# Cross-attention and a routed expert layer: the second norm moves to ScalarE, and block 0 goes ahead of the last attention slot

## What is computed

```python
def reference(x, ctx_1024, mask, Wq, bq, Wk, bk, Wv, bv, norm_scale, w_router, w_up, w_down):
    x = x + xattn(layernorm(x), ctx_1024, mask, Wq, bq, Wk, bk, Wv, bv)
    return x + ffn(layernorm(x), norm_scale, w_router, w_up, w_down)

def ffn(x, norm_scale, w_router, w_up, w_down):
    xn = x * norm_scale * rsqrt(mean(x ** 2) + 1e-6)
    scores = xn @ w_router.T
    top, idx = top_k(scores, 2)
    weights = softmax(top)
    u, gate = split(moe_linear(xn, idx, w_up))
    down = moe_linear(u * silu(gate), idx, w_down)
    return sum(down * weights) + x
```

## Time and profile before

| | |
|---|---|
| median of 3 runs | 450.25 us (450.22 to 450.42) |
| the profiled execution | 450.19 us |
| its span, first to last instruction | 448.3 us |
| PE busy | 396.9 us (89%) |
| DVE busy | 345.0 us (77%) |
| ACT busy | 267.5 us (60%) |
| POOL busy | 252.8 us (56%) |
| mean granted TensorE clock | 0.964 |

### The profile page before, as it was taken

The page is one execution under the profiler, slowest core; times in us unless marked ns, Lnnn a source line. Parts: engine busy times, 40 slices in busy tenths (PEclk is TensorE's granted clock), DMA queues, the critical chain, the costliest instruction groups (busy, mean ns, idle before and its releaser), DMA issues. The chain is left out here.

```text
span 448.3 us, 10369 instructions
## 1 busy us (share of the span) xinstructions
PE 396.9 (89%) x2742; PEld 361.5 (81%) x2742; DVE 345.0 (77%) x1453; ACT 267.5 (60%) x642; POOL 252.8 (56%) x347
## 2 busy tenths in 40 slices
PE   2598999999999999999999999777989999999960
PEld 1598999999999999999999989756878788888750
DVE  2486888898898898898898898655776676777772
ACT  1165666656656656656656645424757677777750
POOL 1063244566566566566566574436777766566670
PEclk9989999999999999999999999776999999999995
DMA  4954473483483483483483350231223643338526
GB/s 125 326 150 171 166 264 95 162 281 97 171 280 105 165 283 104 164 283 107 159 284 111 154 168 21 59 86 30 74 84 102 158 117 87 84 90 285 193 67 217
DMA packets 60824, 68.66 MB, mean 153 GB/s; under 512 B 6096, under 2 KB 52320, under 8 KB 60768
## 3 DMA queue, kind: packets, MB, share of 16 engines
q1 hardware_dynamic: 56192, 58.52, 40.7%
q0 software_dynamic: 4544, 9.38, 6.3%
q10 hardware_dynamic: 32, 0.10, 0.1%
HBM read 54.41 MB, written 13.57 MB: 152 GB/s over the span
## 5 line engine op out<-in xcount | busy, mean ns | idle before, releaser
L1280 PE MATMUL ps<-attention,ctx_sb 128*128 128x128 f32 (+1 forms) x832 | 116.4, 282 | 10.5 <-ACT attention L704 4.8
L1280 PEld LDWEIGHTS ps<-attention,ctx_sb 128*128 128x128 f32 (+1 forms) x832 | 103.6, 195 | 17.7 <-issue 11.2
L631 POOL DMA_INDIRECT parts<-mbias,blk_x x78 | 77.8, 997 | 39.7 <-ACT mbias L771 31.5
L704 ACT ACTIVATE attention<-ps 128x512 f32<-128x512 f32 x96 | 56.5, 597 | 36.4 <-PE ps L1262 32.4
L537 POOL TENSOR_TENSOR rstd<-ve,minus_half 128x2 f32<-128x2 f32 x32 | 26.8, 837 | 90.0 <-DVE ve L894 90.0
L574 POOL DMA_INDIRECT rows_in<-kept,place x64 | 67.5, 1054 | 13.2 <-issue 12.7
L1262 PE MATMUL ps<-ident,attention 128*128 128x128 f32 (+1 forms) x416 | 68.4, 281 | 0.0
L838 DVE CUSTOM_DVE_ANT_0 attention<-ps,mbias 128x1608 f32<-128x1608 f32 x32 | 58.6, 1830 | 4.3 <-issue 4.3
L678 ACT ACTIVATE attention<-attention,ebias 128x1601 f32<-128x1601 f32 x32 | 52.0, 1624 | 10.9 <-DVE ebias L856 10.7
L1185 DVE SCALAR_TENSOR_TENSOR ctx_sb<-ctx_sb,ps 128x256 f32<-128x256 f32 x78 | 32.8, 420 | 33.0 <-ACT ctx_sb L758 32.2
L1246 PE MATMUL ps<-ctxt_high,gt_high 128*128 128x402 f32 x128 | 48.3, 378 | 5.0 <-DVE ctxt_low L980 3.0
(11 more groups left out here) (132 smaller groups left out, 828.4 us busy)
## 6 DMA issues: line engine op xcount, KB each, us to landing
ctxt_in<-ctx_cols SPq DMA_DIRECT2D x16, 800.5 KB
mbias<-mbias_dram SPq DMA_DIRECT2D x16, 800.5 KB, 5.7
ctx_sb<-ctx_rows SPq DMA_DIRECT2D x16, 768.0 KB
blk_x<-rows_in SPq DMA_DIRECT2D x78, 65.0 KB, 1.9
attention<-parts SPq DMA_DIRECT2D x8, 512.0 KB, 5.2
x_in<-x SPq DMA_DIRECT2D x16, 128.0 KB, 4.7
wup_in<-w_up_t SPq DMA_DIRECT2D x8, 256.0 KB, 5.1
out<-base_all SPq DMA_DIRECT2D x8, 256.0 KB, 3.1
```

Source lines behind the costliest of these rows:

```text
L631: pool.indirect_dma_start(parts, bass.IndirectOffsetOnAxis(ap=blk_x[:, m % XR, D:D + 1].bitcast(I32), axis=0), blk_y[:, m % YR], None).the ...
L704: act.activation(probs_t[:, g * BANK:(g + 1) * BANK], ps_turn[:, g % 2], ACT.Copy).then_inc(s_pt_act, 1)
L1280: last = pe.matmul(ps_o[:, 0:P], ctx_sb[0:n, j, t], probs_t[0:n, t * P:(t + 1) * P], start=t == 0, stop=t == KT - 1)
```

## The change

Three things are done at once.

1. **The second norm.** Instead of three passes of DVE and one of POOL over a row, ACT makes both rows with one activation each, out = scale * x1 + bias with a scale and a bias per token: the normalised row straight into kept (`norm_unit`, twice 128 values) and the skip sum (`add_skip`). The coefficients are made on POOL behind the power: shift2, the roots times minus the mean (128x2), and scale2, the root plus one (128x1). DVE makes minus the mean (128x1), and the two variances in one instruction instead of two. norm_unit(u - 2) is ACT's first work in slot u, and PE now turns kept instead of xn2. norm_scale goes into the router weights, once, by DVE ahead of slot 0 (PE waits for it, `s_wr`), and into the up weights as they are split; norm_scale is loaded as 128x1 instead of 128 copies of its row.
2. **Smaller ones on DVE.** The logits aren't copied any more: `best` and `best_index` read them in PSUM, both ahead of the big maximum instead of behind it, and what waited for the copy (`s_lg`) now waits for the index. The two choices are marked by one instruction instead of two (`gates_hot`). The last expert's up weights are split in slot 30 instead of 31.
3. **The order.** Slot 31, the last one with attention, comes behind step 0, and the three behind it behind steps 2, 5 and 8 instead of 1, 4 and 7; the last ranking goes from step 10 to 11. PE's waits for the last turned probabilities go from `before_steps` to step 2. The blocks' hidden rows lie in the mask's buffer instead of that of the context, which slot 31 still reads.

```diff
-    LATE_SLOTS = [1, 4, 7]
-    LAST_RANK = 10
+    LATE_SLOTS = [0, 2, 5, 8]
+    LAST_RANK = 11
...
-        inner = ctx_sb[:].rearrange("p a t d -> p (a t d)")[:, 0:4 * 2 * H].rearrange("p (s j h) -> p s j h", s=4, j=2)
+        inner = mbias[:].rearrange("p a n -> p (a n)")[:, YR * D:YR * D + 4 * 2 * H].rearrange("p (s j h) -> p s j h", s=4, j=2)
...
-            for u in range(UNITS):
+            for u in range(UNITS - 1):
                 slot(u // 4, u % 4)
             before_steps()
             for m in range(NB + 3):
                 step(m)
                 if m in LATE_SLOTS:
-                    slot(PAIRS, LATE_SLOTS.index(m))
+                    u = UNITS - 1 + LATE_SLOTS.index(m)
+                    slot(u // 4, u % 4)
...
             def slot_first(i, k):
                 u = 4 * i + k
-                if is_unit(u - 2):
-                    pool.wait_ge(s_y, u - 1)
-                    pool.tensor_tensor(base_all[:, bass.ds(u - 2, 1)],
-                                       x1[:, (k - 2) % 4:(k - 2) % 4 + 1], y[:, (k - 2) % 2:(k - 2) % 2 + 1],
-                                       ALU.add).then_inc(s_base, 1)
...
                     pool.wait_ge(s_ve2, u)
-                    wait(pool, s_xn2, u - 1)
-                    pool.tensor_tensor(rstd2[:], ve2[:], minus_half[:], ALU.pow).then_inc(s_rs2, 1)
+                    wait(pool, s_xn2, u - 2)
+                    wait(pool, s_base, u - 2)
+                    pool.tensor_tensor(rstd2[:, j], ve2[:], minus_half[:], ALU.pow).then_inc(s_rs2, 1)
+                    pool.wait_ge(s_rs2, u)
+                    pool.wait_ge(s_mm, u)
+                    pool.tensor_tensor(shift2[:, j], rstd2[:, j], minus_mean[:].broadcast_to([P, 2]), ALU.mult)
+                    pool.tensor_tensor(scale2[:, j], rstd2[:, j, 0:1], ones[:, 0:1], ALU.add).then_inc(s_coef, 1)
...
+            def norm_unit(u):
+                act.wait_ge(s_coef, u + 1)
+                if u >= KEPT:
+                    act.wait_ge(s_scat[u % KEPT], 16 * TOP_K * (u // KEPT))
+                act.activation(kept[:, u % KEPT, :, 0:D], x1[:, u % RING:u % RING + 1].broadcast_to([P, TOP_K, D]),
+                               ACT.Identity, bias=shift2[:, u % 2, 1:2], scale=rstd2[:, u % 2, 1:2]).then_inc(s_xn2, 1)
+            def add_skip(u):
+                act.activation(base_all[:, u], x1[:, u % RING], ACT.Identity, bias=shift2[:, u % 2, 0:1],
+                               scale=scale2[:, u % 2]).then_inc(s_base, 1)
...
+                if is_unit(u - 2):
+                    norm_unit(u - 2)
                 if k % 2 == 1 and is_unit(u + 3):
                     split_ctxt(i + 1, k // 2)
...
                     act.activation(xnt[:, k % 2], ps_misc[:, 0:P], ACT.Copy).then_inc(s_rtc, 1)
-                    act.activation(kept[:, (u - 2) % KEPT, :, 0:D], xn2[:, k % 2:k % 2 + 1].broadcast_to([P, TOP_K, D]),
-                                   ACT.Copy).then_inc(s_keep, 1)
+                    add_skip(u - 2)
...
-                dve.tensor_scalar(ve2[:, 0:1], mv2[:, 1:2], LN_EPS, None, ALU.add)
-                dve.tensor_scalar(ve2[:, 1:2], mv2[:, 1:2], 1.0 + RMS_EPS, RMS_EPS * LN_EPS, ALU.mult,
-                                  ALU.add).then_inc(s_ve2, 1)
+                dve.scalar_tensor_tensor(ve2[:], ve_mul[:], mv2[:, 1:2], ve_add[:], ALU.mult, ALU.add).then_inc(s_ve2, 1)
+                dve.tensor_scalar(minus_mean[:], mv2[:, 0:1], -1.0, None, ALU.mult).then_inc(s_mm, 1)
-            def ln2_centre(i, kk):
-            def ln2_norm(i, kk):
-            def rms_norm(i, kk):
-            def take_logits(i, kk):
...
-                dve.max(top[:], logits[:]).then_inc(s_top, 1)
+                dve.max(top[:], ps_misc[:, 0:E]).then_inc(s_top, 1)
...
-                dve.max_index(top_i[:], top[:], logits[:]).then_inc(s_topi, 1)
+                dve.max_index(top_i[:], top[:], ps_misc[:, 0:E]).then_inc(s_lg, 1)
...
-                if k == 3 and is_unit(u):
+                if k == (3 if i < PAIRS - 1 else 2) and is_unit(u):
                     split_up_weights(i)
...
                 if is_unit(u - 2):
-                    take_logits(i, k - 2)
+                    best(i, k - 2)
+                    best_index(i, k - 2)
                 if is_unit(u + 1):
                     maximum(*following)
...
             ln1(0, 1)
             dve.wait_ge(s_consts, N_CONSTS)
+            dve.tensor_scalar(wr_sb[:], wr_in[:], norm_col[:], None, ALU.mult).then_inc(s_wr, 1)
...
-                    pe.transpose(ps_misc[:, 0:P], xn2[:, (k - 2) % 2], ident[:]).then_inc(s_rt, 1)
+                    pe.transpose(ps_misc[:, 0:P], kept[:, (u - 2) % KEPT, 0, 0:D], ident[:]).then_inc(s_rt, 1)
...
             pe.wait_ge(s_consts, N_CONSTS)
+            pe.wait_ge(s_wr, 1)
...
                 if is_block(m - 2):
                     pe.wait_ge(s_h, m - 1)
+                    if m == 2:
+                        pe.wait_ge(s_pt_dve, UNITS)
+                        pe.wait_ge(s_pt_act, 3 * UNITS)
...
                 pe.wait_ge(s_max, UNITS)
-                pe.wait_ge(s_pt_dve, UNITS)
-                pe.wait_ge(s_pt_act, 3 * UNITS)
                 pe.wait_ge(s_owner, 1)
                 load_owners(0)
                 turn_block(0)
```

102 lines of the change are left out of this document (45 added, 57 removed).

## The result

The change makes the kernel **slower: 460.14 us** (458.23 to 460.92, 4 runs) against 450.34, a ratio of 1.020 [1.017, 1.024]. The forecast was 454.1 us with a range to 458.0: right in its sign, short by 6 us. The profiled execution took 460.92 us, 10.7 more than that of before, its span 459.2.

A forecast was written before the change was run, and what follows sets the result against it. PE was taken to set the time, through its waits and clock. Start 2.5, attention slots -2.0 and boundary 3.4 gave +3.9 on 450.2: 454.1 us, spread 451.5 to 456, to 458 with low clock and late coefficients.

The forecast's parts named there:

- Start: Slot 0: PE's scores for unit 1 wait for scaled router weights, 4.1 us later, less 1.6 us: +2.5 us.
- the bound on POOL's small operations: Coefficients on POOL: its two new small operations take at most 226 ns each, from a 128x8 sum.
- The rival of late coefficients: Attention slots: POOL's small ones take twice their bound, PE waits some 0.1 us at 30 places, +3 us; chance 0.10.
- Attention slots: Even slots: the next queries' turn starts 0.17 us earlier in 12 slots, -2.0 us; L995's 3.5 us stay.
- ACT's price: ACT's two new activations add 0.64 us per unit, 20 us in all, costing PE nothing while two covers hold.
- Boundary: Slot 30's end to block 6's products: 34.0 us against 30.6, with 10.3 us idle for block 0: +3.4 us.
- waits of PE for the activation that writes kept: Sign that the prediction is wrong: PE waiting for ACT's normalised row.
- Behind that, the shift stays.: Behind block 6: PE is busy throughout, so the delay stays as it is.
- The low clock: Boundary rival: the clock stays low after the 10.3 us idle stretch, +3.0 us, 457.1 us; chance 0.18.
- The covered start: Start rival: the start's wait is covered, so its 2.5 us fall away, 451.6 us; chance 0.10.
- the faster case: Even slots: DVE's relief reaches both PE waits, 6.7 us instead of 2.0, giving 449.4 us; chance 0.10.
- The early load: Boundary rival: block 0 is loaded early, so the slot hides nothing, 10.3 us less, 443.8 us; chance 0.05.

The follow-up runs named there:

- second trace of the change: The change as it is, run again beside other kernels: 460.39 us, ratio 1.019.
- early row: Against the change, ACT makes the normalised row of the three late slots ahead of the block step before the slot: 457.16 us, 1.014.
- early load: Against the change, the row ends are signalled by themselves and only block loads wait for the owners: 451.62 us, 1.003.
- repaired split: Against the change, DVE's split of the context in slots 2 and 4 waits for POOL's coefficients: 456.22 us, 1.016.
- PE kept busy: Against the change, 60 products of the unit matrix while PE waits for block 0: 459.71 us, 1.017; with 46 products 457.90 us, 1.017.
- 46 products with the early row: The change with the late slots' row made early on ACT and 46 unit-matrix products while PE waits for block 0: 456.05 us, 1.013.
- the half that paid: The new normalisation alone, in the old order, against the kernel before: 449.85 us, 0.999; with both start repairs 447.15 us, 0.992.
- the other half: The kernel before with only the new order of slots and blocks and what it needs: 455.77 us, 1.013.

## Why the prediction was right in sign and wrong in size

- **Start, forecast +2.5.** The first steps hold: PE at 26.00 (26.2 forecast), slot 2 late by 2.6. What failed is the bound on POOL's small operations, 226 ns each. Two of them took 1.42 and 1.57 us beside the split, and slots 2 and 4 gave 1.3 us more. The row of a 128x8 sum gave the time of such an operation alone. I looked at what DVE has ahead of the coefficients, not at what it does beside them. (In the second trace of the change it is worse, 2.1 us, by the power of 2.79 us.) The rival of late coefficients thus came true in 2 slots and not in 30: in the other even slots the row never made PE wait.
- **Attention slots, forecast -2.0.** An even slot took 0.18 us less (0.17 forecast), and the waits at L995 kept their 3.5 us. With two odd slots of 7.96 and 8.09 us instead of 7.68, slot 6 to the end of slot 30 gave back 1.5 us. The rule that I weighed against it, the Trainium skill's cycles for a PSUM source (VectorE: DVE Perf Modes, The TRN2 errata), shows nothing here: MAX8 and the index, now from PSUM, took 0.17 us each, against 0.17 and 0.16 from SBUF.

```profile
214.21 0.17 DVE L928 MAX8 top<-ps 128x8 f32<-128x8 f32 x1 [0.16 <-issue]
...
214.50 0.17 DVE L933 FIND_INDEX8 top_i<-top,ps 128x8 uint32<-128x8 f32 x1
```

- **ACT's price.** 595 and 483 ns for the two activations (0.59 and 0.46 forecast), 19.1 us in all (20 forecast). That its covers hold was right until slot 30, but for slots 2 and 4 (waits of 0.34 and 0.39 us), and wrong behind it.
- **Boundary, forecast 34.0 us to block 6's products, +3.4.** It took 321.85 - 285.07 = 36.8 us, +6.2. Term by term: idle 10.6 (10.3); two turns and block 0's products 3.15 (2.6); the row 0.96 (1.0); slot 31 7.9 (8.3); from block 2's turn on **14.1 (11.8)**. The step that failed: "Less work of DVE in slot 32 and two blocks in flight take off most of the 3.15 us and the low-clock window behind it, about 4.5 us." They took off 2.2, so this term was 2.3 us too small. I had seen that slot 31's row stands on ACT behind a block step and counted 1.0 us for it; slots 32 and 33 have the same place on ACT, and I counted nothing. These waits were 1.02 and 0.94 us, and the sign "waits of PE for the activation that writes kept" came true. From block 2's turn to block 6's products the kernel with the early row took 11.95 us, close to the 11.8, while the early load and the repaired split, with the waits and a clock of 1.00, took 13.1. So of the 2.3 us 1.2 are the row's place on ACT and 1.0 the clock of 0.86.
- **"Behind that, the shift stays."** It grew from 8.5 to 10.7 us: 1.0 up to block 20, where the clock was 0.95, and 1.2 behind, in small losses that no experiment isolates.
- **Rivals.** The low clock came, in slot 31 and further on; against PE kept busy it costs 3.3 us from block 0 to 2, of which 0.8 to 2.5 reached the end. I had slot 31 at 8.3 us and so most of that in the sum; what I had not was the 0.86 and 0.95 behind it. The Trainium skill has the rule that I gave for it in the section behind the one that the prediction names (TensorE: Matmul & The Clock Gate, A second HAM failure mode: psum-queue depth-cycling), and tells it of one kernel: frequent micro-idles between groups of products made the engine alternate between its two rates. It agrees with the change's 0.86 and with the early row's 1.00. It doesn't explain the early load and the repaired split, which have the same gaps and 1.00, nor the 46 products with the early row, which have 0.94 from block 2 to 8 and 0.96 to block 20 without these gaps. The covered start did not come, nor the faster case: PE's second wait didn't shrink at all. The early load did not come either. Making it come was worth 8.5 us, but it took 7.1 us off block 0's turn and not the 10.3 that the rival named.
- **The sum.** Forecast 2.5 - 2.0 + 3.4 = 3.9. Measured in the profile 3.8 - 1.5 + 6.2 + 2.2 = 10.7 (the last is the growth behind block 6).

## What to carry to other kernels

When work moves to another engine, price each place where it will stand, not one slot times their number: the row cost PE nothing in 27 slots, 0.3 to 0.4 us in two and 1 us in each of the three where it fell behind a block step. When a slot is taken out of a cover, first shorten what it covered: signalling the row ends by themselves was worth 8.5 us here, more than any other repair. And test a change of several parts by its parts: the half that paid was hidden by two costs at the start, and the other half cost 5.6 us by itself. Gains of repairs measured one by one don't have to add up: here they make 19.5 us and gave 15.9 together.
